# A four-block transformer kernel: its opening pieces are spread evenly, its value products move to the middle of a slot, and its closing slot network is cut and filled with extra products

## What is computed

```python
q, k, v = x @ Wq.T, ctx @ Wk.T, ctx @ Wv.T          # 16 heads of 16
a = softmax(0.25 * (q k^T * tau + delta))           # 2048 x 1601 for each head
x = x + (a v) @ Wo.T
x = x + weight * (x @ expert_w[top1].T)             # 8 experts, the best of each token
x = x + tanh([window attention context, x] @ Wc.T)  # a window of 256 context rows
# slot network, 64 slots
h = gelu([x, slot_mean] @ w1 + b1); alpha = softmax of the 8 largest of (h @ w2 + b2)
si = (alpha^T x) / alpha.sum()
S_new = GRU cell of (si @ Wih.T, slot_init @ Whh.T)
y = layernorm(S_new + attention(S_new)) * ln_g + ln_b
out = alpha @ (y @ wvp + bvp) @ wo + bo             # added to x
```

## Time and profile before

| | us |
|---|---|
| median of three executions | 1170.94 (1169.78 to 1175.02) |
| the profiled execution | 1169.3 |
| its span, first to last instruction | 1167.6 |
| PE busy | 1003.9 (86%) |
| DVE busy | 791.9 (68%) |
| ACT busy | 575.9 (49%) |
| POOL busy | 67.7 (6%) |
| mean granted TensorE clock | 0.931 of full |

### The profile page before, as it was taken

The page is one execution under the profiler, slowest core; times in us unless marked ns, Lnnn a source line. Parts: engine busy times, 40 slices in busy tenths (PEclk is TensorE's granted clock), DMA queues, the critical chain, the costliest instruction groups (busy, mean ns, idle before and its releaser), DMA issues.

```text
span 1167.6 us, 13692 instructions
## 1 busy us (share of the span) xinstructions
PE 1003.9 (86%) x4812; PEld 409.0 (35%) x4812; DVE 791.9 (68%) x1774; ACT 575.9 (49%) x1045; POOL 67.7 (6%) x86
## 2 busy tenths in 40 slices
PE   4678999999899989988999989899899898695556
PEld 2433333223433334323333344333333343343424
DVE  3478878877677777776677787766677867444232
ACT  3243766666545456665445465664455566201210
POOL 5143000000000000001000000000000000100000
PEclk7888999999999989999999899998999999987665
DMA  4982500001000000010000000010000000100602
GB/s 127 165 163 79 130 15 15 1 15 32 1 14 1 14 1 15 1 33 19 13 3 1 14 1 15 1 51 1 15 1 14 1 14 1 50 1 0 175 26 72
DMA packets 36144, 38.19 MB, mean 33 GB/s; under 512 B 7406, under 2 KB 32719, under 8 KB 35815
## 3 DMA queue, kind: packets, MB, share of 16 engines
q1 hardware_dynamic: 34812, 36.76, 12.8%
q10 hardware_dynamic: 1184, 0.30, 0.1%
q0 software_dynamic: 80, 0.26, 0.1%
HBM read 23.42 MB, written 8.13 MB: 27 GB/s over the span
## 4 chain that ended last, share of the span: by engine, by line
issue 47%; PE 30%; DVE 10%; DMA 4%; ACT 2%; SPq 2%; DVEq 2%; POOL 2%; POOLq 1%; ACTq 0%
PE ps_o L922 8%; PE ps_e L1088 7%; PE ps_m L828 7%; DVE mx L1233 6%; PE ps_e L812 2%; DMA xres<-in_x 1%; SPq L420 1%; PE ps_m L1151 1%; ACT probs L707 1%; PE ps_m L1037 1%; PE ps_m L1040 1%; DMA x<-xres 1%; POOL xres L623 1%; POOL rstd L566 1%; PE ps_m L950 1%
## 5 line engine op out<-in xcount | busy, mean ns | idle before, releaser
L1233 DVE TENSOR_REDUCE mx<-ps_m 128x1 f32<-128x401 f32 x1102 | 580.4, 568 | 217.2 <-PE ps_m L828 209.5
L707 ACT ACTIVATE probs<-ps_e 128x512 f32<-128x512 f32 (+1 forms) x832 | 472.7, 597 | 373.6 <-PE ps_e L1088 372.4
L828 PE MATMUL ps_m<-k_stack,q_stack 99*128 99x401 bf16 x1102 | 345.6, 344 | 46.4 <-DVE mx L1233 39.5
L1088 PE MATMUL ps_e<-q_stack,k_stack 101*128 101x512 bf16 (+1 forms) x832 | 327.1, 393 | 8.2 <-ACT probs L707 6.2
L922 PE MATMUL ps_o<-probs,v_heads 128*32 128x512 f32 (+1 forms) x1664 | 225.9, 616 | 0.0
L1088 PEld LDWEIGHTS ps_e<-q_stack,k_stack 101*128 101x128 bf16 (+1 forms) x832 | 82.8, 100 | 300.3 <-ACT probs L707 208.3
L828 PEld LDWEIGHTS ps_m<-k_stack,q_stack 99*128 99x128 bf16 x1102 | 110.1, 100 | 170.0 <-DVE mx L1233 109.3
L991 PE MATMUL ps_m<-expert_w,xnT 128*128 128x512 f32 x256 | 129.6, 607 | 16.3 <-DVE xb L1368 16.3
L1368 DVE SCALAR_TENSOR_TENSOR xb<-ps_m,hot,xb 128x256 f32<-128x256 f32 x112 | 54.2, 484 | 17.6 <-PE ps_m L991 8.4
L991 PEld LDWEIGHTS ps_m<-expert_w,xnT 128*128 128x128 f32 x256 | 47.2, 195 | 47.8 <-DVE xb L1368 24.7
L922 PEld LDWEIGHTS ps_o<-probs,v_heads 128*32 128x32 f32 (+1 forms) x1664 | 33.1, 109 | 64.4 <-issue 57.0
(11 more groups left out here) (232 smaller groups left out, 628.7 us busy)
## 6 DMA issues: line engine op xcount, KB each, us to landing
...
```

What stands on the lines that cost most here:

```text
L707: act.activation(probs[0:n, k % 2, h, :], ps_e[h % 2][0:n, :], ACT.Exp).then_inc(s["exp_done"], 1)
L828: pe.matmul(ps_m[:, (UNITS * n1 + u) % RING, 0:SPLIT], qst[0:MAX_ROW, g, h, P * t:P * t + P], kst[0:MAX_ROW, HG * g + h, QUARTER_START[q]: ...
L1088: pe.matmul(ps_e[h % 2][0:n, :], kst[0:ROWS, HG * g + h, P * st:P * st + n], qst[0:ROWS, g, h, :], start=True, stop=True).then_inc(s["qk_r ...
L1233: dve.tensor_reduce(mx[:, q, col:col + 1], ps_m[:, (UNITS * n1 + u) % RING, 0:SPLIT], AX.X, ALU.max)\
```

## The change

1. **Start.** The statistics of chunk 0 (L 0) come ahead of the first key block. Five small loads on ACT's queue become one (`cond`, prepared on the host; 7 values for each partition), beside `lenS2`. POOL starts delta's lower parts behind the window load and the first `scale_shift`, where it made their first subtraction ahead of both.
2. **Opening.** `BESIDE` is built of 31 pieces, one at every 2.4 units. A projection's second half is a piece of its own (F). W and X are split in two. DVE's half of V, M and W has a number of its own (v, U and u, w), some units behind PE's.
3. **Attention.** `units_at` deals 1, 1, 2, 1 max units to the quarters where it dealt 1, 2, 1, 1, and `pv` is made behind the second quarter of a slot.
4. **Last `behind`.** Six, five, five and four products of 512 columns by the identity, whose results nothing reads (`keep_warm`), stand ahead of four of PE's waits; ahead of a fifth stands `slot_state` (slot_init by Whh, wvp by wo, wvp's bias product), ahead of the third also `slot_bias`. The slot network's loads are issued right behind the last score product.
5. **Close.** The Whh products, ln_g, ln_b, bvp and the separate product by wo are gone from the chain (they are in wvo and in a bias row), and `keep_warm` stands at six places.

```diff
-START = [("D",), ("C",), ("K", 0, 0), ("L", 0), ("K", 1, 0), ("N", 0), ...
+START = [("D",), ("C",), ("L", 0), ("K", 0, 0), ("K", 1, 0), ("N", 0), ...
...
+for i, piece in enumerate(PIECES):
+    BESIDE += [(1 + 12 * i // 5, step) for step in piece]
+    for step in piece:
+        if step[0] == "T":
+            BESIDE += [(12 * i // 5 - 11, ("L", step[1])), (12 * i // 5 - 4, ("N", step[1]))]
+        if step[0] == "V":
+            BESIDE += [(3 + 12 * i // 5, ("v", step[1]))]
+        if step[0] == "M":
+            BESIDE += [(12 * i // 5 - 6, ("U",)), (3 + 12 * i // 5, ("u",))]
+        if step[0] == "W":
+            BESIDE += [(6 + 12 * i // 5, ("w",))]
+BESIDE += [(76, ("P", "Q", 3, 1))]
...
-    return units[:1] if h == 0 else units[1:1 + len(units) - 3] if h == 1 else units[len(units) - 4 + h:len(units) - 3 + h]
+    return units[h:h + 1] if h < 2 else units[2:-1] if h == 2 else units[-1:]
...
             for c in range(1, NC):
                 chunk_loads(c, True)
-            store_x3(NC - 1)
-
+            sp.wait_ge(s["qk_ready"], HG * SLOTS * NC)
             for dst, src in slot_loads:
                 sp.dma_start(dst, src).then_inc(s["ld_slot"], 16)
+            store_x3(NC - 1)
...
+            def keep_warm(n, out):
+
+                for _ in range(n):
+                    pe.matmul(out, ident[:], wc[:, 0:KT, :], start=True, stop=True)
+
+            def slot_state():
+
+                pe.wait_ge(s["ld_slot"], 16 * len(slot_loads))
+                product(ps_e[0][0:NS, :], slotT, whhT[:, :, 0:2 * D], last=False)
+                product(ps_e[1][0:NS, 0:D], slotT, whhT[:, :, 2 * D:3 * D]).then_inc(s["p_gh"], 1)
+                for k in range(KT):
+                    mm = product(ps_o[:, D * k:D * k + D], wvpT[:, :, P * k:P * k + P], wos)
+                mm.then_inc(s["p_wvo"], 1)
...
                 yield AT["t1a"]
+                if c == NC - 1:
+                    keep_warm(6, ps_m[:, 0, :])
...
                 yield AT["t2a"]
+                if c == NC - 1:
+                    slot_state()
...
-                    if k or c:
-                        pv(c, k - 1)
+                        if h == 1 and (k or c):
+                            pv(c, k - 1)
...
+            keep_warm(2, ps_m[:, 0, :])
             transpose_slots(vec, "p_si", "p_siT_ps")
-            pe.wait_ge(s["ld_slot"], 16 * len(slot_loads))
             pe.wait_ge(s["p_siT"], 1)
-            product(ps_m[0:NS, 0, :], sT, wihT[:, :, 0:2 * D], last=False)
-            product(ps_m[0:NS, 0, :], slotT, whhT[:, :, 0:2 * D], first=False)
-            product(ps_m[0:NS, 1, 0:D], sT, wihT[:, :, 2 * D:3 * D])
-            product(ps_m[0:NS, 2, 0:D], slotT, whhT[:, :, 2 * D:3 * D]).then_inc(s["p_gi"], 1)
+            product(ps_e[0][0:NS, :], sT, wihT[:, :, 0:2 * D], first=False)
+            product(ps_m[0:NS, 1, 0:D], sT, wihT[:, :, 2 * D:3 * D]).then_inc(s["p_gi"], 1)
+            keep_warm(4, ps_m[:, 0, :])
             transpose_slots(s_new, "p_snew", "p_snT_ps")
...
-            product(ps_m[0:NS, 1, 0:D], sT, wvps).then_inc(s["p_sv"], 1)
-            transpose_slots(vec, "p_svb", "p_svT_ps")
-            pe.wait_ge(s["p_svT"], 1)
-            product(ps_m[0:NS, 2, 0:D], sT, wos).then_inc(s["p_svo"], 1)
+            pe.wait_ge(s["p_wvo_sb"], 1)
+            product(ps_m[0:NS, 2, 0:D], sT, wvo, first=False).then_inc(s["p_svo"], 1)
+            keep_warm(1, ps_m[:, 0, :])
...
-            dve.tensor_scalar(y_ln, y_ln, small[:, 7:8], small[:, 10:11], ALU.subtract, ALU.mult)
-            dve.drain()
-            dve.tensor_tensor(y_ln, y_ln, ln_g, ALU.mult)
-            dve.drain()
-            dve.tensor_tensor(y_ln, y_ln, ln_b, ALU.add).then_inc(s["p_y"], 1)
+            dve.tensor_scalar(y_ln, y_ln, small[:, 7:8], small[:, 10:11], ALU.subtract, ALU.mult).then_inc(s["p_y"], 1)
```

164 lines of the change are left out of this document (96 added, 68 removed), and 4 rows, old and new, of the table PIECES.

## The result

The changed kernel takes **1154.9 us** (median of 4 runs, 1154.2 to 1160.7), the kernel before, measured beside it, 1173.0 (1169.8 to 1175.0). The ratio is **0.987, 95% interval 0.984 to 0.990**: 1.3% faster, where 1134 (3.1%) was forecast and 1154 was the upper end of the range.

| stretch | before | after | change | forecast |
|---|---|---|---|---|
| start to the first max product | 46.6 | 48.1 | +1.5 | -3.4 |
| opening, to the first score product | 67.9 | 71.8 | +3.9 | -0.4 |
| attention, to the last value product | 889.9 | 896.7 | +6.8 | -5 |
| last `behind`, close and output | 163.3 | 136.9 | -26.4 | -28.1 |

The account below looks back on a forecast made before the run. PE sets the pace in the attention; in the opening PE and DVE wait by turns; late stretches run at low clock. Terms -3.4 - 0.4 - 5 - 14.5 + 0.5 - 10.6 - 3.5 = -36.9 give 1134 us; range 1118 to 1154 (0.8).

Parts of the forecast that it names:

- Start, -3.4 forecast: Start: scalars come 4 us earlier, and everything queued behind delta on SP 3.4 us earlier; bounds 0 and 6.
- POOL starts its window load some 3.9 us earlier, makes the same steps, and only its 3.0 us subtraction moves: Start, on POOL: statistics end near 12.1 us, the shift near 15.6, delta's steps at 23.4.
- Opening, -9.5 + 7.1 + 2 forecast: Opening: loop 67.7 to 58.5 us, 7.1 of new wait at its end, 2 for low clock; together -0.4, between -5 and +8.
- The stall: End of the opening: the first score product waits for the row of maxima behind the last query block's store, +7.1 us.
- two passes, 0.86: Opening: half a block costs PE 0.86 us at full clock, a piece 1.3 against DVE's 1.2; the ring takes up the rest.
- Attention, -5 forecast: Attention: plain slots +3, `take_o` waits +1, `normalise` slots -6, other gains -15, fourth-quarter pieces +12; between -15 and +10.
- The sign that I gave for failure: The prediction fails if the clock is low in the last `behind`, or PE's waits on maxima in a chunk exceed 20 us.
- Last `behind`, -14.0 forecast with the loads: Last `behind`: low-clock windows run at full clock, -14.5, between +5 and -15; slot loads behind the load of `xres`, +0.5.
- the clock does not hold through the last `behind`: Rival, last `behind`: transpositions and waits behind each filler let the clock fall, the 14.5 are lost, 1148 us; chance 0.09.
- Close, -10.6 forecast: Close: GRU products -4.3, products and transpositions between -1.9, layer norm -0.4, products and transpositions after it -4.0.
- Output, -3.5 forecast: Output: 32 passes took 14.0 us at half clock; the first half now at full clock, -3.5, between 0 and -7.
- the first (1154, the attention's order loses its gains): Rival, attention: fourth-quarter pieces cost what others gain, plain slots lose 0.1 each; 15 us more, 5 in the close; chance 0.14.

Follow-up runs that it names:

- With the waits filled: Changed kernel with window transfer later, maxima load first, attention repeats and opening fillers: 1124.2 us; with four opening products for nine and one more close filler: 1120.2 us.
- The filled waits: Changed kernel with max products repeated at TensorE's longest waits in chunks 1 to 3: 1137.7 us; as many repeats where it hardly waits: 1183.9 us.
- the two held orders: Repeated max products at each order's own longest waits: changed kernel's order 1137.7 us; changed kernel with the attention order of before 1140.7 us.

## Why the forecast was off, step by step

**Start, -3.4 forecast, +1.5 measured.** The loads came when I said. The step that failed is "POOL starts its window load some 3.9 us earlier, makes the same steps, and only its 3.0 us subtraction moves": POOL's first drain lets nothing pass until that load has landed. Before, the subtraction lay ahead of that stand; now it lies behind it. Before, the stand cost nothing either, since the transfer landed at 19.0 (3.4 us from its issue), just when the statistics were ready:

```profile
15.60 0.95 POOL L603 DMA_DIRECT2D o_unnormed<-in_ctxT  x1 [2.41 <-issue]
19.21 0.42 POOL L564 TENSOR_TENSOR var_e<-mv,eps 128x4 f32<-128x4 f32 x1 [2.67 <-DVE mv L1219]
```

With the transfer moved away the first max product comes at 42.0. I had even written that the subtraction moved "out of a wait that it filled", and asked only what the wait was worth, not what it was for.

**Opening, -9.5 + 7.1 + 2 forecast, +3.9 measured.** The stall was right in place, cause and size (6.6 for 7.1). The loop was not: -2.2 (67.9 to 65.7), where -9.5 was summed. The term that failed is "two passes, 0.86" and with it PE's 1.3 us per piece: I priced the products at the full clock. TensorE is at half clock for 17 to 21 us of the opening, before and after, behind its waits for DVE and ACT. In that time a projection's half takes 1.9 us and not 1.0, and the ring of three cannot take that up. In the changed kernel, behind the masks:

```profile
75.54 0.52 PE L869 MATMUL ps_m<-k_stack,q_stack 99*128 99x401 bf16 x1 [3.76 <-DVE mx L1292]
75.85 1.91 PE L829 MATMUL ps_e<-xnT,expert_w 128*128 128x512 f32 x2
...
110.57 1.02 PE L829 MATMUL ps_e<-xnT,expert_w 128*128 128x512 f32 x2
```

With the waits filled the loop is 59.0, and 58.5 was the forecast. The count was right for a clock that the kernel did not have.

**Attention, -5 forecast, +6.8 measured.** Slot by slot the sum held: plain slots 3.13, the `normalise` slot 3.1 (3.2 forecast), chunk 0 shorter by 2.0, and 2 us less waiting in chunk 3. What failed is that the sum had no term for the clock within the chunks. I read "at a clock of 0.99" from chunk 3 as a property of the attention. It was a property of that order: the changed one has 24 us of half clock in that chunk where 7 were before. The sign that I gave for failure, waits on maxima above 20 us in a chunk, looked at their total (8.5) and said nothing of the clock. The filled waits show the clock as the cause of the loss: order and clock-held order differ by 17 us, the two held orders by 3. Why one order lets the clock fall more than another, no run here settles.

**Last `behind`, -14.0 forecast with the loads, -9.2 measured** (from the last value product to the first step of the close 111.0 before, 101.8 after). Six fillers take 5.3 us, as sized:

```profile
1024.75 5.31 PE L968 MATMUL ps_m<-wc,ident 128*128 128x512 f32 x12
1032.76 1.09 PE L993 MATMUL ps_m<-ident,xn 128*128 128x128 f32 x8 [2.70 <-DVE xn L1284]
```

The clock did not hold throughout. Behind the first and third filled waits, eight transpositions and a wait for their copies follow, and there it stands at 0.50 for 6.8 and 3.4 us:

```profile
1033.00:1035.00 2.00, 1.23 (x12) 1.02 (x10) 0.00 (x0) 1.07 (x2) 0.00 (x0) 1.00 0.35 50
1035.00:1041.80 6.80, 6.80 (x19) 4.51 (x20) 2.02 (x11) 0.23 (x1) 0.00 (x0) 0.50 0.00 0
...
1089.60:1093.00 3.40, 3.06 (x7) 2.52 (x8) 0.00 (x0) 0.24 (x1) 0.00 (x0) 0.50 0.00 0
```

That is the rival "the clock does not hold through the last `behind`", in two places of four. The rule beside which it stood (the Trainium skill, "TensorE: Matmul & The Clock Gate", Part 4: PE-mode transpose: transpositions do not count as busy in the same way) does not decide it alone. In both places 2.70 and 1.47 us of waiting lie ahead of the transpositions. In the other two the same eight transpositions stand behind no wait (at 1076.75) and behind one of 0.71 us (at 1104.82), and the clock held there. What the transpositions add to a wait, no run here shows.

**Close, -10.6 forecast, -10.3 measured** (33.5 to 23.3 us). **Output, -3.5 forecast, -6.9 measured**, to the end of the span: I did not trust the clock to stay up in it. It stays: 32 passes in 7.1 us, where they took 14.0. The error was on the careful side: I took the clock to fall halfway. In these runs a clock that was up stayed up through the output's products back to back, and a clock that was down had not risen in 14 us of them. The last `behind` gave 4.8 us less than forecast and the output 3.4 more, so it is in part luck that the tail as a whole came within 1.7.

**Rivals.** The nearest in time was the first (1154, the attention's order loses its gains), and the reason given for it was wrong: plain slots and exposed pieces did not cost more. The range failed since three terms missed in one direction: the opening and the attention within the bounds given for each, the start outside them (0 to 6 less).
